# First self attention of a two-block decoder: scores from halves of the array's rows, no staging copies, weighted sums in pairs, projections from split rows

## The reference, cut to what matters

```python
# N_HEADS = 16, D_HEAD = 64; x is (2, 1024, 256), wq, wk, wv are (256, 1024)
h = _layernorm(x, ln1_g, ln1_b)
q = (h @ wq).reshape(B, S, 16, 64)
k = (h @ wk).reshape(B, S, 16, 64)
v = (h @ wv).reshape(B, S, 16, 64)
attn = jax.nn.softmax(jnp.einsum("bihd,bjhd->bhij", q, k) * 64 ** (-0.5), axis=-1)
x = jnp.einsum("bhij,bjhd->bihd", attn, v).reshape(B, S, 1024) @ wo + bo + x
```

## Time and profile before

| | us |
|---|---|
| median of 3 runs | 2029.41 (2028.31 to 2030.17) |
| the profiled execution's own time | 2027.02 |
| its span | 2025.3 |
| PE busy | 1851.6 (91% of the span) |
| DVE busy | 1157.2 (57%) |
| ACT busy | 781.4 (39%) |
| POOL busy | 879.0 (43%) |

### The profile page before, as it was taken

The page is one execution under the profiler, slowest core; times in us unless marked ns, Lnnn a source line. Parts: engine busy times, 40 slices in busy tenths (PEclk is TensorE's granted clock), DMA queues, the critical chain, the costliest instruction groups (busy, mean ns, idle before and its releaser), DMA issues. The chain is left out here.

```text
span 2025.3 us, 27798 instructions
## 1 busy us (share of the span) xinstructions
PE 1851.6 (91%) x8972; PEld 1078.1 (53%) x8972; DVE 1157.2 (57%) x2195; ACT 781.4 (39%) x1300; POOL 879.0 (43%) x767
## 2 busy tenths in 40 slices
PE   4999999999999999979899999996798976898799
PEld 1444444444444444438555577885444434665678
DVE  4666666666666666633566433244688853687601
ACT  2344444444444443441344313221266663344340
POOL 2366666666666666661122300111146655366110
PEclk9999999999999999989999899997699998999899
DMA  1422222232323232203000001103244421000001
GB/s 52 107 62 53 61 54 67 62 70 62 70 62 70 62 70 62 63 24 94 24 1 1 1 3 48 28 10 53 51 70 77 87 48 28 9 1 1 29 16 42
DMA packets 64798, 93.99 MB, mean 46 GB/s; under 512 B 20992, under 2 KB 47132, under 8 KB 64703
## 3 DMA queue, kind: packets, MB, share of 16 engines
q1 hardware_dynamic: 60351, 86.20, 18.9%
q0 software_dynamic: 4352, 6.56, 1.5%
HBM read 22.84 MB, written 2.24 MB: 12 GB/s over the span
## 5 line engine op out<-in xcount | busy, mean ns | idle before, releaser
L1181 POOL TENSOR_TENSOR x<-x,sa_p_buf 128x1024 f32<-128x1024 f32 x192 | 455.2, 2371 | 165.7 <-ACT sa_p_buf L1029 157.7
L1029 ACT ACTIVATE sa_p_buf<-sa_score 128x512 f32<-128x512 f32 x512 | 277.7, 595 | 304.7 <-PE sa_score L956 304.5
L1092 DVE TENSOR_REDUCE sa_mx<-sa_front 128x1 f32<-128x512 f32 x512 | 319.4, 680 | 98.9 <-PE sa_front L930 98.9
L956 PE MATMUL sa_score<-sa_q_stage,sa_k_stage 128*128 128x512 f32 x1024 | 323.9, 438 | 0.0
L970 PE MATMUL sa_out<-sa_p_buf,sa_v_buf 128*64 128x512 f32 x1024 | 275.7, 617 | 0.0
L956 PEld LDWEIGHTS sa_score<-sa_q_stage,sa_k_stage 128*128 128x128 f32 x1024 | 177.8, 189 | 102.9 <-issue 71.3
L528 ACT ACTIVATE sa_p_buf<-sa_score 128x1024 f32<-128x1024 f32 (+1 forms) x160 | 141.1, 938 | 89.9 <-PE sa_score L476 89.8
L1668 POOL TENSOR_TENSOR x<-x,bias_out 128x1024 f32<-128x1024 f32 x24 | 55.7, 2348 | 275.5 <-POOLq L1853 239.3
L342 DVE TENSOR_REDUCE sa_mx<-sa_front 128x1 f32<-128x512 f32 (+1 forms) x256 | 155.9, 650 | 26.4 <-PE sa_front L283 23.3
L1181 POOL TENSOR_TENSOR x<-sa_p_buf 128x1024 f32<-128x1024 f32 x32 | 77.9, 2433 | 155.1 <-ACT sa_p_buf L1029 155.1
L1557 POOL TENSOR_TENSOR ca_probs<-ca_s_sb,ca_inv 128x616 f32<-128x616 f32 x64 | 77.9, 1218 | 125.7 <-DVE ca_inv L1491 125.7
(11 more groups left out here) (177 smaller groups left out, 2892.3 us busy)
## 6 DMA issues: line engine op xcount, KB each, us to landing
sa_k_stage<-sa_k_hi SPq DMA_DIRECT2D x64, 256.0 KB, 4.3
sa_q_stage<-sa_q_hi SPq DMA_DIRECT2D x64, 256.0 KB, 5.1
sa_k_stage<-sa_k_lo SPq DMA_DIRECT2D x32, 256.0 KB, 4.8
sa_q_stage<-x SPq DMA_DIRECT2D x32, 256.0 KB, 5.0
x<-in_x SPq DMA_DIRECT2D x8, 512.0 KB, 7.3
sa_q_stack<-sa_hi SPq DMA_DIRECT2D x64, 64.0 KB, 2.3
sa_k_stack<-sa_hi SPq DMA_DIRECT2D x64, 64.0 KB, 2.4
ff_w<-in_L_xattn_ff_w SPq DMA_DIRECT2D x16, 128.0 KB, 2.1
```

What stands on the lines that cost most here:

```text
L956: mm = pe.matmul(score_ps[n % NSCORE][:], k_stage[:, b, j, part, kt * P:(kt + 1) * P], q_stage[:, b, j, part, h * HALF:(h + 1) * HALF], st ...
L1029: nc.scalar.activation(p_buf[:, s % NPB, j, :], score_ps[n % NSCORE][:], ACT.Exp, scale=SCALE).then_inc(exp_done, 1)
L1092: dve.tensor_reduce(mx[:, b, j, qt, half:half + 1], front_ps[bank(item, j)][:], AX.X, ALU.max).then_inc(drained, 1)
L1181: nc.gpsimd.tensor_tensor(acc[:, h], prev, cur, ALU.add).then_inc(added, 1)
```

## The change

1. `q_hi`, `q_lo`, `k_hi`, `k_lo` hold both batches (`[P, B, T]`) and are used for the scores in place; `k_copies`, `q_copies`, the 12 DMAs of a block and both stages are gone.
2. A step's scores are eight matmuls in four pairs (head 0, head 1): hi·hi, hi·lo, lo·hi with 64 rows each, and last two rows of ones against `m_rows`, which hold the negated maxima. In the built program the matmuls with 64 rows fill half of the array's rows (shape 64x128), the ones with two rows a quarter (shape 32x128, at rows 0 and 64).
3. A unit of two steps replaces the step: maxima, scores, maxima, scores, further maxima, other items, then two steps of weighted sums. `lanes` is written anew, for 8 units. `NBANK` goes from 4 to 3 and `NSCORE` from 3 to 4. A pair of maxima waits for both of its banks ahead of both matmuls.
4. q and k are projected from split rows and split weights: `h_hi`, `h_lo`, `w_hi`, `w_lo`, in fp32r, six matmuls for each item where four passes were. ACT and DVE (POOL for the second batch) split the rows once, and the weights once for each group.
5. `front` has an order of its own (`first_front`); POOL's clearing of the stages is gone.
6. In `thin_attention`, `load_top(pool, 1)` moves from before the barrier to behind it.

```diff
@@ thin_attention
                 @block.gpsimd
                 def _(pool):
+                    pool.wait_ge(cleared, B)
+                    load_top(pool, 1)
                     pool.memset(w_out[:], 0.0).then_inc(emptied, 1)
...
     def gpsimd_early(pool, step):
         if step == TT // XCHUNK - 1:
...
             load_top(pool, 0)
-            pool.wait_ge(cleared, B)
-            load_top(pool, 1)
@@ wide_attention
-    NBANK = 4
-    NSCORE = 3
+    NBANK = 3
+    NSCORE = 4
...
-        0: [("n", ("k", 0))],
-        1: [("c", ("m", 5, 1)), ("c", ("m", 6, 1))],
...
+        0: [("c", ("m", 5, 1)), ("c", ("m", 6, 1)), ("n", ("k", 0))],
...
+        7: [("n", ("m", 6, 0)), ("n", ("m", 7, 0)), ("n", ("m", 4, 1)), ("n", ("v", 1))],
...
+    first_front = [("k", 0), ("q", 0), ("k", 1), ("m", 0, 0), ("m", 1, 0), ("m", 2, 0), ("m", 3, 0), ("m", 0, 1), ("m", 1, 1),
+                   ("m", 2, 1), ("m", 3, 1), ("q", 1), ("t", 0), ("v", 0), ("v", 1), ("m", 4, 0), ("m", 5, 0), ("m", 6, 0),
+                   ("m", 7, 0), ("m", 4, 1)]
@@ tensor
+                def project(g, b, item):
+                    a = 0 if item[0] == "q" else 1
+                    fr = front_ps[bank(item)]
+                    if item == ("k", 0):
+                        pe.wait_ge(w_split, g + 1)
...
+                    parts = [(ws[:, a, kd, :], hs[:, kd, tokens(c)]) for kd in range(KD)
+                             for ws, hs in ((w_hi, h_hi), (w_hi, h_lo), (w_lo, h_hi))]
+                    for n, (ws, hs) in enumerate(parts):
+                        mm = pe.matmul(fr[:], ws, hs, start=(n == 0), stop=(n == len(parts) - 1))
+                    mm.then_inc(front_full, 1)
+                def maxima(g, b, item):
+                    _, qt, half = item
+                    wait_free(g, b, item, 0, ("q", qt // QH), ("k", half))
+                    wait_free(g, b, item, 1)
+                    for j in range(G):
+                        r = slice(dh * j, dh * j + dh)
+                        pe.matmul(front_ps[bank(item, j)][:], q_hi[r, b, qt * P:(qt + 1) * P],
+                                  k_hi[r, b, half * HALF:(half + 1) * HALF], start=True, stop=True).then_inc(front_full, 1)
...
                 def scores(g, b, s):
...
+                    keys, queries = slice(kt * P, (kt + 1) * P), slice(h * HALF, (h + 1) * HALF)
+                    for part, (ks, qs) in enumerate(((k_hi, q_hi), (k_hi, q_lo), (k_lo, q_hi))):
+                        for j in range(G):
+                            r = slice(dh * j, dh * j + dh)
+                            pe.matmul(score_ps[(s * G + j) % NSCORE][:], ks[r, b, keys], qs[r, b, queries], start=(part == 0),
+                                      stop=False, skip_group_check=True)
                     for j in range(G):
-                        for part in range(2):
-                            mm = pe.matmul(score_ps[n % NSCORE][:], k_stage[:, b, j, part, kt * P:(kt + 1) * P],
-                                           q_stage[:, b, j, part, h * HALF:(h + 1) * HALF], start=(part == 0), stop=(part == 1))
-                        mm.then_inc(score_full, 1)
+                        r = slice(dh * j, dh * j + 2)
+                        pe.matmul(score_ps[(s * G + j) % NSCORE][:], one_rows[r, :], m_rows[r, b, queries], start=False,
+                                  stop=True, skip_group_check=True).then_inc(score_full, 1)
...
                 def both(g, b):
+                    for u in range(UNITS):
+                        tops = owned(u, g, b, "m")
+                        for of, item in tops[:1]:
+                            front_item(*of, item)
+                        scores(g, b, 2 * u)
+                        for of, item in tops[1:2]:
+                            front_item(*of, item)
+                        scores(g, b, 2 * u + 1)
+                        for of, item in tops[2:]:
+                            front_item(*of, item)
+                        for of, item in owned(u, g, b, ("q", "k", "v", "t", "den")):
+                            front_item(*of, item)
+                        if u >= 1:
+                            weighted(g, b, 2 * u - 2)
+                            weighted(g, b, 2 * u - 1)
```

More of the change, by code:

```diff
@@ L689, in places @@
                     n += 1
-        order = [(0, item) for s in range(STEPS) for who, item in lanes[s] if who == "n"]
+        order = [(0, item) for item in first_front]
         for i in range(2 * NG):
-            order += [(i + OFFSET[who], item) for s in range(STEPS) for who, item in lanes[s]
+            order += [(i + OFFSET[who], item) for u in range(UNITS) for who, item in lanes[u]
                       if 0 <= i + OFFSET[who] < 2 * NG]
@@ L707, in wide_attention @@
     NDRAIN = NSLOT - HALVES
+    assert NSLOT % NBANK == 0
     assert all(FILLED[i + 2, item, k] == n + 2 * NSLOT and FREE[i + 2, item, k][0] == FREE[i, item, k][0]
@@ L732, in is_last, with splits @@
         return isinstance(g, int) and (g, b) == (NG - 1, 1)
+    def splits(g, b):
+        return b == 0 and not (isinstance(g, int) and g == NG - 1)
     def before(g, b):
@@ L746, in owner, with owned @@
         return None if is_last(g, b) else after(g, b)
+    def owned(u, g, b, kinds):
+        return [(owner(who, g, b), item) for who, item in lanes[u] if item[0] in kinds and owner(who, g, b) is not None]
     def sums(s):
@@ L752, in walk @@
     def walk(eng, front, both):
-        front(0, 0)
+        front()
         both(0, 0)
@@ L881, in both @@
                     g2, b2 = after(g, b)
-                    front(g2, b2, g2 + 1 if b2 == 1 and not is_last(g2, b2) else None)
+                    maxima(g2, b2, 0)
+                    if b2 == 1 and not is_last(g2, b2):
+                        sp.wait_ge(drained, drained_count(g2, b2, ("v", 1)))
+                        load_v(g2 + 1)
                 load_qk(0)
@@ new lines, in values @@
+                def values(g, b, item):
+                    fr = front_ps[bank(item)]
+                    if item == ("v", 0):
+                        pe.wait_ge(wv_in, (g + 1) * DMA)
+                    for t in range(4):
+                        at = b * T + (item[1] * 4 + t) * P
+                        for kd in range(KD):
+                            mm = pe.matmul(fr[:, t * GD:(t + 1) * GD], hT[:, kd, at:at + P], wv[:, kd, :],
+                                           start=(kd == 0), stop=(kd == KD - 1))
+                    mm.then_inc(front_full, 1)
@@ L972, in weighted @@
                     mm.then_inc(pv_done, 1)
-                def denominators(g, b, h):
-                    pe.wait_ge(added, lin(g, b, NADD, (KT - 1) * (h + 1)))
-                    wait_free(g, b, ("den", h), 0)
-                    for j in range(G):
-                        mm = pe.matmul(front_ps[bank(("den", h))][64 * j:64 * j + 64, :], ones[:, 0:64], acc[:, h, j, :],
-                                       start=True, stop=True)
-                    mm.then_inc(front_full, 1)
-                def front(g, b):
-                    for s in range(STEPS):
-                        for who, item in lanes[s]:
-                            if who == "n":
-                                front_item(g, b, item)
@@ L988, in both, with front @@
-                def both(g, b):
-                    for s in range(STEPS):
-                        scores(g, b, s)
-                        if s >= 2:
-                            weighted(g, b, s - 2)
-                        elif not is_first(g, b):
-                            weighted(*before(g, b), s + STEPS - 2)
-                        for who, item in lanes[s]:
-                            of = owner(who, g, b)
-                            if of is None:
-                                continue
-                            if item[0] == "den":
-                                denominators(*of, item[1])
-                            else:
-                                front_item(*of, item)
+                def front():
+                    for item in first_front:
+                        front_item(0, 0, item)
@@ L1063, in both @@
                             else:
-                                front_item(*of, item)
+                                high(*of, item)
+                        if u == UNITS - 2 and splits(g, b):
+                            split_w(g + 1)
                     if is_last(g, b):
@@ L1076, in front_item @@
                     if kind in ("q", "k"):
[L1077 to L1083 removed]
+                        low(g, b, item)
                     elif kind == "v":
```

283 lines of the change are left out of this document (126 added, 157 removed), and 6 rows, old and new, of the table lanes.

## The result

The changed kernel takes **2061.51 us** (median of 4 runs, 2059.55 to 2065.73), the kernel before on the same chip 2029.41: a ratio of 1.0162, 95% interval 1.0141 to 1.0182. It is 1.6% slower. (A fourth run of the kernel before was a slow one, 2193.62 us, and is left out of its median and of the ratio.) The forecast was 2031.0 with a range of 1974 to 2047, so it lies above both. The profiled execution took 2061.71 us, its span 2060.0 us.

The account below looks back on a forecast made before the run. PE's own work was taken to bound the steady part. Terms -23 - 51 + 80 - 15 + 4 + 11 + 1 - 5.7 = +1.3 on 2027.0 us gave 2028.3 profiled, 2031 us as median; range 1974 to 2047.

Parts of the forecast that it names:

- (f): Steady part, three banks: a pair of maxima needs the bank of the pair ahead; new waits +4 us, bounds 0 and 25.
- Rival B: Banks: two reciprocals on DVE in units 2, 3, 6 and 7 hold PE; +26 us, 2057 us, chance 0.11.
- (d): Steady part: the two-row matmuls change the array's shape, 25 changes a block at 0.20 us; +80 us.
- Rival A: Scores: the change between 64 and 32 rows is free (1975 us) or half price (1999 us); chance 0.30.
- C: Rival on the scores: the two matmuls with two rows don't overlap; +59 us, 2090 us, chance 0.05.
- (b): Steady part: maxima and scores share one shape, sums come once a unit; 3.2 us of changes saved a block, -51 us.
- (a): Projections: four passes of 0.43 us become six matmuls of 0.227 us; 1.4 us a block, -23 us.
- (e): Behind a den item, the second pair of maxima no longer waits until ACT has taken the sums; -15 us.
- (g): Front, first projection to first scores: splits, projection round trips and pairs waiting for two banks; +11 us, bounds 6 and 16.
- (h): End of the stage: two steps of sums instead of one remain behind the last scores' exponentials; +1 us.
- (i): Barrier: without the eight DMAs ahead of it, it can close at DVE's end; -5.7 us, bounds -7 and -3.
- (j): DMAs, staging and POOL's clearing gone: no gain, PE wasn't waiting for them; extra ACT and DVE splits beside PE's work.

Follow-up runs that it names:

- the first experiment: The changed kernel with row maxima joined by four one-input reductions instead of two-input maximum, copy and two-input subtraction: 2027.48 us, ratio 0.9999 to the kernel before.

## Why the prediction was wrong

**(f), the new waits, is the step that failed**: "So it is covered, by 0.2 us", +4 us with bounds of 0 and 25. The first experiment puts it at 31 us: 863.84 against 832.78 us from first scores to last den, by the join alone. In the changed kernel PE stands 20 times ahead of its maxima in that stage, 22 us in all; the rest is the lower clock. The round trip was costed from the reduction's 0.68 us, rightly: with the lock gone PE has no wait. What was left out is what else stands between reductions. The joins were costed nowhere, as instructions of 0.17 us; that was their price in the kernel before because all of them but one fell between additions. In the changed kernel scores come in twos, so POOL often makes two additions on end, 4.9 us, and the join of a first half falls under such a pair. The order of the instructions was read for PE and not for DVE against POOL.

The Trainium skill has the rule, and I hadn't weighed it: SBUF — State Buffer, "Who interferes with whom", says that a DVE instruction in a two-port mode and a GpSimd instruction (POOL is GpSimd) exclude each other for the whole of the one that starts first, and that one with two inputs in SBUF contends with a GpSimd instruction that reads SBUF, as an addition does. Of a reduction it says that on trn2 it never contends. The trace agrees: each of the 30 locked maxima and copies ends 0.02 to 0.03 us behind an addition, and no reduction is longer under one.

**Rival B** gave 2057 us and its sign, PE idle ahead of L916 with DVE as releaser, is what the profile shows, 1.5 us a block. Its cause is nevertheless refuted: the reciprocals stand untouched in the first experiment, where PE waits for nothing. A rival can hit the number and the sign with the wrong culprit.

**(d), the two-row matmuls**, +80: right in kind, and in size as a price of the changes. In the changed kernel's lines above three distances are longer than the plain 0.23 us: 0.32 ahead of the two-row pair, 0.44 behind it and 0.34 behind the maxima that follow. The excess is 0.41 us for the two changes into the pair and out of it, 0.2 each. Taken away, the pair gives back only 58 us: with 64 rows throughout the 0.34 behind such maxima stays, and PE is busy for 726.6 of 730 us, not for all. Rival A (1975 us) is out, C too: pairs stand 0.23 us apart.

**(b), shape changes saved**, is not refuted. The distance behind the maxima that follow weighted sums is 0.34 us as well, but there it is the second half of a change that (b) counts in full, 0.10 us ahead of the maxima (0.53 for 0.43 behind the sums) and 0.10 behind:

```profile
541.93 0.50 PE L916 MATMUL sa_front<-sa_k_hi,sa_q_hi 64*128 64x512 f32 x2
542.27 0.40 PE L962 MATMUL sa_score<-sa_q_hi,sa_k_hi 64*128 64x512 f32 x2
```

Added up over a block of the first experiment, all that lies beyond the plain distances (0.23 us for an fp32r pair, 0.43 for an fp32 one, 0.11 for a product of v) is 9.0 us; (b) and (d) leave 4.4 + 5.0 = 9.4. **(a)** is a little smaller: the six matmuls stand 0.233 us apart and not 0.227, so 20 us for 23. (a), (b), (d) and (e) together are -9 us or -0.56 a block: 52.86 - 0.56 = 52.30 us, and 52.29 was measured without the lock. The agreement to 0.01 us is luck, since (a) is off by 0.1 us a block and the changes by 0.4 the other way; that a block is near 52 us without the lock is not.

**(g), the front**: +11, measured 1.3 + 13.5 = 14.8, inside 6 to 16. The waits of pairs for both banks, forecast at 4.5, are 3.6 to 5.8 us of it. **(h)**: from the last scores' start to the last den, 5.3 us before and 6.3 after, +1.0 for +1. **(i)**: -5.7, measured -5.74 (the working has a slip: 1399.2 - 1393.4 is 5.8, and the row has PE's start at 1399.45). **(j)**: right for PE, though the DMA traffic fell from 93.99 to 43.69 MB, and wrong for DVE, whose split of the weights met the lock once the join had pushed it back.

One term had no place in the sum. The first scores come while PE runs at 1.2 GHz: from there on it did so for 9.3 us in the changed kernel and for 17.3 in the first experiment, and for 0.1 us in the kernel before. By an estimate that work takes twice as long at 1.2 GHz (a projection's matmuls stand 0.43 us apart there and 0.23 at 2.4 GHz), the lower clock cost 5 and 9 us there. It is why the third line of the table shows +0.3 us for the first experiment, where -8 is left of the forecast without (f).

With 31 us for (f) in place of 4 the sum is 2028.3 + 27 = 2055; the front's 4 us more and some 5 for the lower clock ahead of the steady part bring 2064, and 6 us less in stretches whose code is the same leave 2058. The profiled execution has 2061.7. The rest fits (f) being somewhat more than 31 us, since the first experiment, against which it is read, ran longer at the lower clock at the stage's start; by the medians the join is worth 34.

## What to carry to other kernels

When a change moves small instructions of DVE whose operands are in SBUF, lay them beside POOL's list: under an addition of 2.4 us each can grow from 0.17 to 2.3 us, and all that is queued behind it on DVE is late. A group's mean of 1.2 us for 8 elements is the sign; the page's list of the costliest groups doesn't show it, since the group is small. Look for it in the trace before the change too, by the longest of a group and not by its mean. The cure is either the form (a reduction) or the place, and what is left of the chain must not reach the next addition, or it is locked as long. Where DVE has time to spare behind the locked instruction, as with the scaling of 2.51 us, nothing has to be cured.

## What was not expected of the hardware

- Locked under POOL's additions: a maximum of two SBUF inputs (1.88 us), a copy (2.28), a multiplication by a number (1.69), a two-input subtraction (2.36, 2.26), a scaling of two SBUF inputs (2.51). Not locked, under the same additions: reductions, reciprocals (0.92 us), copies of v out of PSUM (0.66), and the low parts of q and k, with one of two inputs in PSUM (0.69).
- Short waits of PE can cost more than themselves: behind 1.18 and 1.31 us in one block PE ran at 1.2 GHz for 6.8 us. In the first experiment, without such waits, the steady part ran at 2.4 GHz throughout. But so it did in the version with 64 rows and the locks left in, which waited for 37 us of 730: what makes the difference isn't shown.
- The same code takes different times: from PE's first scores to its last in the second block's self attention the runs took between 234.2 us (11.1 of them at 1.2 GHz) and 243.7 (39.8 of them). Differences of a few us in the total are read from stages, not from medians.
- With 64 rows throughout, a pair of maxima behind a pair of the same shape is still followed by 0.34 us, where scores in that place are followed by 0.23. Why stays open; it wasn't tried.
